# Key softmax on one core: value products in 512-column halves at every second score tile, written out over the batch items

## The reference

```python
q = split_heads(x @ Wq)      # 16 heads of 16; B*H, S, dh
k = split_heads(x @ Wk)
v = split_heads(x @ Wv)
scores = jnp.einsum('bqd,bkd->bkq', q, k) / jnp.sqrt(jnp.asarray(D, x.dtype))
attn = jax.nn.softmax(scores, axis=-1)
out = jnp.einsum('bkq,bkv->bqv', attn, v)
...
z = z @ Wo
z = _l2_normalize(z)
z = z @ Wff
z = _l2_normalize(z)
z = jax.nn.gelu(z, approximate=False)
```

## Time and profile before

| what | value |
|---|---|
| median of 3 runs | 1923.31 us (1920.8 to 1923.41) |
| the profiled execution | 1923.6 us, span of its instructions 1921.8 us |
| granted TensorE clock over the span | 0.982 of full speed |
| TensorE busy | 1806.0 us (94%) |
| VectorE busy | 1440.7 us (75%) |
| ScalarE busy | 1524.3 us (79%) |
| GpSimd busy | 670.2 us (35%) |
| exponentials of the stage, first and last start | 1239.0 and 1835.5 us |

### The profile page before, as it was taken

One profiled execution on the slowest core, in us unless ns is written; L12 is line 12 of the kernel. 1 busy time (PEld: TensorE's weight loads), 2 busy tenths in 40 slices (PEclk: granted clock), 3 DMA queues, 4 the chain that ended last, 5 costly groups with the idle time before them and its releaser, 6 DMA issues. The chain is left out here.

```text
span 1921.8 us, 45100 instructions
## 1 busy us (share of the span) xinstructions
PE 1806.0 (94%) x16198; PEld 1202.4 (63%) x16198; DVE 1440.7 (75%) x2675; ACT 1524.3 (79%) x4461; POOL 670.2 (35%) x778
## 2 busy tenths in 40 slices
PE   6999999999999999699999989899999999999995
PEld 5888888888888888459999988622222222222232
DVE  7577777777777777346666655699999999989946
ACT  6677777777777777348888865699999999999964
POOL 2343444444444444304675630022222222222222
PEclk9999999999999999999999999999999999999998
DMA  7222333333333233151101006633543443335002
GB/s 175 46 62 62 62 62 62 62 62 62 62 60 63 62 61 56 37 151 47 44 15 44 18 21 165 194 45 45 78 57 45 62 65 52 45 61 73 2 21 68
DMA packets 139782, 121.74 MB, mean 63 GB/s; under 512 B 78875, under 2 KB 111535, under 8 KB 139567
## 3 DMA queue, kind: packets, MB, share of 16 engines
q1 hardware_dynamic: 139567, 118.88, 31.8%
HBM read 77.29 MB, written 41.53 MB: 62 GB/s over the span
## 5 line engine op out<-in xcount | busy, mean ns | idle before, releaser
L1925 DVE TENSOR_REDUCE s_neg_max<-s_ring 128x1 f32<-128x1024 f32 x512 | 580.8, 1226 | 23.2 <-PE s_ring L1839 22.9
L1887 ACT ACTIVATE s_prob<-s_ring,s_neg_max 128x1024 f32<-128x1024 f32 x512 | 570.5, 1115 | 13.6 <-DVE s_neg_max L1925 13.3
L1852 PE MATMUL s_acc<-s_prob,s_v_norm 128*32 128x256 f32 x4096 | 327.8, 393 | 11.9 <-ACT f_zT_all L1879 9.8
L1839 PE MATMUL s_ring<-f_stack 128*128 128x512 bf16 x1024 | 312.2, 387 | 11.5 <-ACT s_prob L1887 10.2
L1908 POOL TENSOR_TENSOR s_row_inv<-s_row_sum,s_neg_one 128x4 f32<-128x4 f32 x128 | 128.8, 1007 | 410.8 <-ACT s_prob L1887 410.8
L1852 PEld LDWEIGHTS s_acc<-s_prob,s_v_norm 128*32 128x32 f32 x4096 | 81.6, 108 | 229.4 <-issue 213.5
L592 POOL TENSOR_SCALAR a_relu_ring<-a_qT 128x512 f32<-128x512 f32 x64 | 98.6, 1557 | 343.5 <-ACT a_qT L463 316.1
L1839 PEld LDWEIGHTS s_ring<-f_stack 128*128 128x128 bf16 x1024 | 58.4, 97 | 234.8 <-ACT s_prob L1887 219.2
L492 ACT ACTIVATE a_prob<-a_psum,a_neg_max 128x128 f32<-128x128 f32 x512 | 179.8, 402 | 21.4 <-DVE a_neg_max L697 21.4
L740 DVE SCALAR_TENSOR_TENSOR a_att<-a_psum,a_keep_cols,a_num_s 128x128 f32<-128x128 f32 x256 | 72.2, 345 | 133.2 <-ACT a_num_s L518 133.2
L1278 ACT ACTIVATE x_prob<-x_psum,x_neg_max 128x77 f32<-128x77 f32 x512 | 160.8, 337 | 14.1 <-DVE x_neg_max L1435 14.0
(11 more groups left out here) (198 smaller groups left out, 4047.6 us busy)
## 6 DMA issues: line engine op xcount, KB each, us to landing
f_stack<-qk_thirds SPq DMA_DIRECT2D x256, 128.0 KB, 6.1
segment_values<-a_v_stage SPq DMA_DIRECT2D x64, 256.0 KB, 3.5
a_v_pos<-segment_values SPq DMA_DIRECT2D x512, 32.0 KB
qk_thirds<-p_third SPq DMA_DIRECT2D x16, 768.0 KB, 8.5
a_x_in<-in_x_dram SPq DMA_DIRECT2D x16, 256.0 KB, 3.2
a_x_res<-in_x_dram SPq DMA_DIRECT2D x32, 128.0 KB, 2.8
after_attention<-a_normed SPq DMA_DIRECT2D x32, 128.0 KB, 2.4
x_x_in<-after_attention SPq DMA_DIRECT2D x32, 128.0 KB, 2.1
```

Of the source, the lines that this page charges most:

```text
L1839: last = pe.matmul(ring[n % 3][:, f * HALF:(f + 1) * HALF], k_stack[:, slot, j, kt * P:(kt + 1) * P], q_stack[:, slot, j, f * HALF:(f + 1) ...
L1852: last = pe.matmul(acc[32 * j:32 * j + 32, s], v_norm[:, step // KT % 2, step % 4, j, :], prob[:, step % 4, j, s], start=step % (2 * KT) = ...
L1887: act.activation(prob[:, step % 4, j, :], ring[n % 3][:, :], ACT.Exp, bias=neg_max[:, step % 2, j:j + 1], accum_out=row_sum[:, step % 4, j ...
L1925: dve.tensor_reduce(neg_max[:, step % 2, j:j + 1], ring[n % 3][:, :], AX_X, ALU.max, negate=True).then_inc(max_ready, 1)
```

## The change

Three things change in `emit_key_softmax`, and nothing outside it. First, `values` works on a half of 512 columns and runs only behind the scores of j = 1 (left half) and j = 3 (right half), for the step two before. Second, the output copy is made in two halves with semaphores of their own: the left by ScalarE behind the exponential of j = 0 in the second step of the next chunk, the right by VectorE behind the maximum of j = 3 of that step; the first value block of each half waits for its own copy. Third, all five engines' programs are written out over the four batch items, so that every wait is against a constant.

```diff
-    PIECE = S // 4
...
+        half_done = [sem("left_done"), sem("right_done")]
+        zT_ready = [sem("left_taken"), sem("right_taken")]
...
         @block.sync
         def _(sp):
-            def batch(b, first=0):
-                for group in range(first, GROUPS):
-                    sp.wait_ge(scores_done, b * TURNS + (group - 1) * (TURNS // GROUPS))
-                    load_stacks(sp, parts, b, group, group % 2, stacks, stack_landed)
-
-            batch(0, first=2)
-            with sp.Fori(1, B) as b:
-                batch(b)
+            for b in range(B):
+                for group in range(GROUPS):
+                    if b > 0 or group >= 2:
+                        sp.wait_ge(scores_done, b * TURNS + (group - 1) * (TURNS // GROUPS))
+                        load_stacks(sp, parts, b, group, group % 2, stacks, stack_landed)
 
         @block.tensor
         def _(pe):
-            def scores(b, step, j, first):
-
-                n = step * 4 + j
+            def scores(b, step, j):
+                n = b * TURNS + step * 4 + j
                 slot, kt = (step // KT) % 2, step % KT
                 if n >= 3:
-                    pe.wait_ge(exp_done, b * TURNS + n - 2)
-                elif not first:
-                    pe.wait_ge(exp_done, b * TURNS + (TURNS - 1 - (TURNS - 1 - n) % 3) - TURNS + 1)
+                    pe.wait_ge(exp_done, n - 2)
...
-            def values(b, step, piece, first):
-
-                s = slice(piece * PIECE, (piece + 1) * PIECE)
-                if piece == 0:
-                    pe.wait_ge(vnorm_ready, b * STEPS + step + 1)
-                    if step % (2 * KT) == 0 and not (first and step == 0):
-                        pe.wait_ge(zT_ready, b * ZC + step // (2 * KT))
+            def values(step, half):
+                s = slice(half * HALF, (half + 1) * HALF)
+                chunk = step // (2 * KT)
+                if half == 0:
+                    pe.wait_ge(vnorm_ready, step + 1)
+                if step % (2 * KT) == 0 and chunk > 0:
+                    pe.wait_ge(zT_ready[half], chunk)
                 for j in range(4):
                     last = pe.matmul(acc[32 * j:32 * j + 32, s], v_norm[:, step // KT % 2, step % 4, j, :],
-                                     prob[:, step % 4, j, s], start=step % (2 * KT) == 0 and piece % 2 == 0,
+                                     prob[:, step % 4, j, s], start=step % (2 * KT) == 0,
                                      stop=step % (2 * KT) == 2 * KT - 1, skip_group_check=True)
-                if piece == 3:
-                    last.then_inc(pv_done, 1)
+                last.then_inc(half_done[half], 1)
...
                     for j in range(4):
-                        scores(b, step, j, first)
-                        if step >= 2 or not first:
-                            values(b, step - 2, j, first)
+                        scores(b, step, j)
+                        if b * STEPS + step >= 2 and j % 2 == 1:
+                            values(b * STEPS + step - 2, j // 2)
...
         @block.scalar
         def _(act):
+            def take_left(chunk):
+                act.wait_ge(half_done[0], (chunk + 1) * 2 * KT)
+                act.copy(zT_all[:, chunk // ZC, chunk % ZC, 0:HALF], acc[:, 0:HALF]).then_inc(zT_ready[0], 1)
...
-                        if step % (2 * KT) == 1 and j == 2 and not (first and step == 1):
-                            take_outputs(b, step // (2 * KT) - 1)
+                        if n // 4 % (2 * KT) == 1 and j == 0 and n // 4 > 1:
+                            take_left(n // (8 * KT) - 1)
+            take_left(B * ZC - 1)
...
         @block.vector
         def _(dve):
-            with dve.Fori(0, B) as b:
+            def take_right(chunk):
+                dve.wait_ge(half_done[1], (chunk + 1) * 2 * KT)
+                dve.tensor_copy(zT_all[:, chunk // ZC, chunk % ZC, HALF:S], acc[:, HALF:S]).then_inc(zT_ready[1], 1)
+
+            for b in range(B):
                 for step in range(STEPS):
                     for j in range(4):
-                        n = step * 4 + j
-                        dve.wait_ge(scores_done, b * TURNS + n + 1)
+                        n = b * TURNS + step * 4 + j
+                        dve.wait_ge(scores_done, n + 1)
                         dve.tensor_reduce(neg_max[:, step % 2, j:j + 1], ring[n % 3][:, :], AX_X, ALU.max,
                                           negate=True).then_inc(max_ready, 1)
+                    if n // 4 % (2 * KT) == 1 and n // 4 > 1:
+                        take_right(n // (8 * KT) - 1)
+            take_right(B * ZC - 1)
```

More of the change, by code:

```diff
@@ L1810, in emit_key_softmax @@
         c_set, v_zeroed = sem("set"), sem("v_zeroed")
-        scores_done, max_ready, exp_done, inv_ready, vnorm_ready, pv_done, zT_ready = (
-            sem("scores_done"), sem("max_ready"), sem("exp_done"), sem("inv_ready"), sem("vnorm_ready"),
-            sem("pv_done"), sem("zT_ready"))
+        scores_done, max_ready, exp_done, inv_ready, vnorm_ready = (
+            sem("scores_done"), sem("max_ready"), sem("exp_done"), sem("inv_ready"), sem("vnorm_ready"))
+        half_done = [sem("left_done"), sem("right_done")]
+        zT_ready = [sem("left_taken"), sem("right_taken")]
         block = ctx.enter_context(nc.Block())
@@ L1842, in scores @@
                 last.then_inc(scores_done, 1)
-            def values(b, step, piece, first):
-                s = slice(piece * PIECE, (piece + 1) * PIECE)
-                if piece == 0:
-                    pe.wait_ge(vnorm_ready, b * STEPS + step + 1)
-                    if step % (2 * KT) == 0 and not (first and step == 0):
-                        pe.wait_ge(zT_ready, b * ZC + step // (2 * KT))
+            def values(step, half):
[5 more added lines that the diff above has]
+                    pe.wait_ge(zT_ready[half], chunk)
                 for j in range(4):
                     last = pe.matmul(acc[32 * j:32 * j + 32, s], v_norm[:, step // KT % 2, step % 4, j, :],
-                                     prob[:, step % 4, j, s], start=step % (2 * KT) == 0 and piece % 2 == 0,
+                                     prob[:, step % 4, j, s], start=step % (2 * KT) == 0,
                                      stop=step % (2 * KT) == 2 * KT - 1, skip_group_check=True)
-                if piece == 3:
-                    last.then_inc(pv_done, 1)
-            def batch(b, first=False):
+                last.then_inc(half_done[half], 1)
+            for b in range(B):
                 for step in range(STEPS):
@@ L1862, in batch @@
                     for j in range(4):
-                        scores(b, step, j, first)
-                        if step >= 2 or not first:
-                            values(b, step - 2, j, first)
[L1867 to L1872, removed]
+                        scores(b, step, j)
+                        if b * STEPS + step >= 2 and j % 2 == 1:
+                            values(b * STEPS + step - 2, j // 2)
+            for step in range(B * STEPS - 2, B * STEPS):
+                for half in range(2):
+                    values(step, half)
         @block.scalar
         def _(act):
[L1876 to L1882, removed]
+            def take_left(chunk):
+                act.wait_ge(half_done[0], (chunk + 1) * 2 * KT)
+                act.copy(zT_all[:, chunk // ZC, chunk % ZC, 0:HALF], acc[:, 0:HALF]).then_inc(zT_ready[0], 1)
+            for b in range(B):
                 for step in range(STEPS):
                     for j in range(4):
-                        n = step * 4 + j
-                        act.wait_ge(max_ready, b * TURNS + n + 1)
+                        n = b * TURNS + step * 4 + j
+                        act.wait_ge(max_ready, n + 1)
                         act.activation(prob[:, step % 4, j, :], ring[n % 3][:, :], ACT.Exp,
@@ L1903, in _ @@
             pool.wait_ge(c_set, 1)
-            with pool.Fori(0, B) as b:
+            for b in range(B):
                 for step in range(STEPS):
                     group, kt = step // KT, step % KT
-                    pool.wait_ge(exp_done, b * TURNS + step * 4 + 4)
+                    n = b * STEPS + step
+                    pool.wait_ge(exp_done, 4 * n + 4)
                     pool.tensor_tensor(row_inv[:, step % 2, :], row_sum[:, step % 4, :], neg_one[:, :], ALU.pow
                                        ).then_inc(inv_ready, 1)
-                    pool.wait_ge(inv_ready, b * STEPS + step + 1)
+                    pool.wait_ge(inv_ready, n + 1)
                     at = group % 2 * HD
                     pool.tensor_tensor(v_norm[:, group % 2, step % 4, :, at:at + HD],
-                                       v_all[:, bass.ds(b, 1), kt, group * 4 * HD:(group + 1) * 4 * HD].rearrange(
-                                           "p b (h d) -> p (b h) d", d=HD),
+                                       v_all[:, b, kt, group * 4 * HD:(group + 1) * 4 * HD].rearrange(
```

(1 more changed line is left out.)

## The result

The changed kernel takes 1927.32 us (median of 7 runs, 1924.29 to 1928.81), before 1920.8 in 7 runs; the ratio is 1.0034, 95% interval 1.0021 to 1.0047. It is slower, by 6.5 us in the medians. The forecast was 1929.0, 5.4 more than before, counted from a profiled execution of 1923.6 us; by the medians the difference is 1.1 us larger than forecast, and the base 2.8 lower.

A forecast was written before the change was run, and what follows sets the result against it. VectorE's row maxima, 1.131 us a turn, were taken to bound the stage before, and a four-turn chain through TensorE after. The terms 21.7 - 5.9 - 9.6 - 0.8 = +5.4 us on 1923.6 gave 1929.0, range 1915 to 1941.

The forecast's parts named there:

- The chain, +21.7: Score-value stage: long value blocks delay even scores, four turns take 4.696 us against VectorE's 4.524; 126 cycles, +21.7 us.
- a sustained spacing below the column count: Rival at value blocks: long passes take less than their columns, or slack is larger; VectorE stays the bound, 1908, chance 0.08.
- a hidden weight load: Rival at value blocks: next score weights load under the longer block, odd turn 1.44 us, total 1917, chance 0.10.
- The copies, -5.9: Seven output copies at chunk ends: 8.8 us of pauses before, 2.9 net with halves, TensorE not waiting; -5.9 us.
- Straight code, -9.6: Batch boundaries: pauses of 0.9, 4.35 and 4.30 us on VectorE's line go when loops are written out; -9.6 us.
- The end, -0.8: Last step: products of 2.46 us and copy of 1.01 become about 1.97 and 0.68 us; -0.8 us.
- The clock's fall: Rival inside the stage: TensorE pauses about 0.37 us each pair, so its clock falls; ten low stretches give 1944, chance 0.10.

The follow-up runs named there:

- five block sizes: Value blocks at odd j of 256, 384, 448, 480 or 512 columns, 512 being the changed kernel; ratios to before 0.9931, 0.9930, 0.9967, 0.9996, 1.0034.
- pieces of 256: Changed kernel with value products back in 256 columns at every turn, copies in halves and straight code kept; 1906.63 us, ratio 0.9931 to before.
- straight code alone: Changed kernel with value products in 256 columns and one output copy of 1024 columns by ScalarE, as before; 1909.34 us, ratio 0.9954 to before.
- 128 and 384 columns: Changed kernel with uneven value blocks, 128 columns at even j and 384 at odd j; ratio 0.9930 to before.
- long blocks alone: Kernel before with only the value products moved to 512 columns at j = 1 and 3; 1936.95 us, ratio 1.0093 to before.

## Why the prediction was right, and where not

- **The chain, +21.7.** Right in mechanism and size. Cycles take 4.70 us, the late start comes once in four turns, and five block sizes lie on the line worked out from the earlier trace rows, each to 1 ns of a cycle, closer than rows read to 10 ns can promise. Between the changed kernel and the one with pieces of 256 the stage differs by 21.1 us: 126 x 0.171 = 21.5, less 7 x 0.16 that falls into the copies, and 0.9 at the stage's start (below), together 21.3.
- **What the Trainium skill says** ("TensorE: Matmul & The Clock Gate", Back-to-back issue gap) of a sustained spacing below the column count is seen in no run here: value passes of 512 float32 columns last 592 ns as in the earlier trace rows, and the blocks take their columns' time. That rival is out, as is the one of a hidden weight load: 1.54 us, not 1.44.
- **The copies, -5.9.** The break is 0.60 us as worked out from the earlier trace rows, and TensorE waits for no copy. In the stage without the chain the halves are worth 4.9 (4.7 worked out). The left half's delay on ScalarE adds nothing, as taken.
- **Straight code, -9.6.** The amount was near, 8.1 in the stage and 8.8 us in time, the reason right only in part. The sentence that failed is that S of turn 256 needs the exponential of three turns before. It needs the one of two turns before, and that was read out at 1532.23 + 0.19 = 1532.42, not at 1531.29. S came 2.0 us after it, and the trace has TensorE's branch of the loop at that time.
```profile
L1868 PEldq COMPARE_BRANCH  x3: 83/3810/3832, 1530.4 to 1833.5; - x3
...
1532.23 0.19 ACT L1887 ACTIVATION_READ_ACCUMULATOR s_prob<-s_ring,s_neg_max 128x1 f32 x1
...
1536.35 1.11 ACT L1887 ACTIVATE s_prob<-s_ring,s_neg_max 128x1024 f32<-128x1024 f32 x1 [2.80 <-DVE s_neg_max L1925]
```

  The two branches that jump back last 3.83 and 3.81 us, the last one, which leaves the loop, 0.08. The first is begun while the engine still works and lasts until 1534.19, 0.26 before S. ScalarE's jump lay under the wait for the maximum, which ended at 1535.09 + 1.23 = 1536.32: it was back at 1535.17. So in this trace TensorE's jump alone makes the late S; no run writes out one of the two alone. In straight code the buffers' count costs 0.98 us at each boundary, and it explains the 0.91 at the first boundary of the earlier trace rows, where no engine but VectorE and GpSimd jumps back. At turns 256 and 384 of the kernel before its wait lies under TensorE's jump, so counting the buffers through while keeping the loops would by this trace save about 0.9 us, not three times that; this wasn't run. The rest of those two pauses, 3.4 and 3.3 us, goes when the loops of TensorE and ScalarE are written out. By the Trainium skill ("Advanced Engine Details and Errata", Control Flow Timing) three branches would cost an estimated 0.3 us. The trace doesn't agree for TensorE's two that jump back, which left it idle 3.06 and 3.04 us. Why they take so long was not tried.
- **The end, -0.8.** Mis-sized: the stretch from the last maximum to the end of the kernel went from 87.6 to 84.5 us, but the halves give only 0.3 to 0.4 of it (84.5 in the kernels with halves at full clock, 84.8 to 84.9 in those with one copy). The term took the last step's 2.46 us from the earlier trace rows, and the granted clock had fallen to 0.50 within them, at 1839.6. At full clock the same four pieces take 1.93 us (the kernel with straight code alone), as long as the two long blocks. The rest of the 3.1 us is the clock: in the kernel before the low stretch went on into the next stage, in the changed one there was none. The kernel with pieces of 256, which has the halves too, had such a stretch in its profile and 87.3 us. The rows are those four pieces, then a window around the stage's end in the kernel before and one in the changed kernel (columns as in the earlier trace rows, the clock is the third number from the end):

```profile
1824.63 1.93 PE L1849 MATMUL s_acc<-s_prob,s_v_norm 128*32 128x256 f32 x32 [1.94 <-POOL s_v_norm L1901]
...
1836.00:1848.00 12.00, 8.59 (x49) 3.62 (x42) 0.00 (x0) 2.59 (x8) 1.40 (x3) 0.72 0.00 1
...
1843.00:1855.00 12.00, 9.38 (x39) 3.65 (x34) 0.69 (x1) 3.57 (x15) 1.41 (x3) 1.00 0.01 2
```

- **The clock's fall.** Not in steady state: with TensorE's pauses the granted clock is 1.00 through 589 us. But the sum had nothing for the start of the stage. Its first ten maxima and the pause behind them cost 2.1 us over VectorE's pace (1.7 of it the pause at turn 10), 0.2 before. Windows of the changed kernel (columns as in the earlier trace rows):

```profile
1240.40:1250.70 10.30, 9.19 (x28) 1.42 (x30) 8.49 (x8) 8.82 (x16) 2.62 (x4) 0.51 0.01 3
1250.70:1840.00 589.30, 523.66 (x2942) 95.87 (x2998) 580.58 (x508) 576.83 (x1006) 162.48 (x250) 1.00 0.36 51
```

So the two profiled spans, 1921.8 and 1925.5, are 3.7 us apart: +8.1 in the stage, -3.1 behind it, -1.3 ahead of it in code that the change doesn't touch. The forecast was 5.4, with +6.2 in the stage (the 0.8 of the end lies behind it); the 1.9 of the start is the difference there. That the sum of the two profiles comes so near is partly luck: 1.9 too little at the start stands against 2.3 more gained at the end, by the clock, and 1.3 ahead of the stage, none of which the forecast had. The medians differ by 6.5.

In the last rows of the stage the copy beside the block is seen as forecast: ScalarE copies the left half while TensorE works on the right, and VectorE's follows (compare):

```profile
1844.97 1.92 PE L1846 MATMUL s_acc<-s_prob,s_v_norm 128*32 128x512 f32 x16 [1.54 <-POOL s_v_norm L1897]
...
1846.11 0.59 ACT L1867 COPY f_zT_all<-s_acc 128x512 f32<-128x512 f32 x1 [2.64 <-PE s_acc L1846]
1846.97 0.69 DVE L1907 COPY f_zT_all<-s_acc 128x512 f32<-128x512 f32 x1 [4.74 <-PE s_acc L1846]
```

Two versions beat both kernels, the one with 128 and 384 columns and the one with pieces of 256: 0.7% faster than before, 1.0% faster than the changed kernel by the two ratios. They can't be told from each other.

## What to carry to other kernels

An engine with spare time can still set the pace, if it hands out its work in lumps: compare its longest turn (here 1.54 us) not with its average load but with the pace plus the slack of the ring of buffers. The slack is here 3 turns less the round through the other engines, 0.23 us, so the limit is 1.131 + 0.23 = 1.36. Beyond it, add up the closed chain that a late start makes. When a loop is written out, look whether an index that counts anew in each round now runs through, and whether the number of turns was a multiple of the number of buffers. Three edits in one change can hide each other: two gained 13 us and one cost about 20 by the ratios. And a duration read from a row counts only at the clock of that row.

## What the runs showed of the hardware

- When TensorE goes from score products (128 columns of weights, bf16) to value products (32, float32) or back, it loses 0.08 to 0.09 us, with blocks of 256 and of 512 columns alike. By single records, the two products of a score tile start 0.226 us apart, the second of them and the block 0.309. The two passes of a block start 0.220 us apart at 256 columns and 0.434 at 512; from the last pass to the next score product it is 0.311 and 0.525.
- A compare-and-branch that jumps back over a batch item's code was recorded on TensorE with 3.8 us, one that falls through with 0.08. On ScalarE the first instruction behind the jump came 2.75 and 2.69 us after the branch began, on VectorE and GpSimd some 0.3. Behind each of TensorE's two jumps stood a stretch of 0.50 clock of 3.4 us, in the kernel before and in the one with the long blocks alone.
- The stretch of 0.50 clock after the start of this stage was 3.4 us long in the kernel before, 10.2 in the changed kernel and in the one with the long blocks alone, and 6.8 in the seven others, in one profiled execution each. That the long blocks lengthen it fits these, but isn't shown.
